# Cross attention with chosen query rows on one core: the order of the loads, of the score weights' spread and of the second choice

## The reference

```python
scores = einsum('bnd,d->bn', x, score_w[0]) + score_b[0]        # x: 8 x 224 x 512
_, topk_idx = top_k(scores, 10)                                  # 10 rows of each input
sparse = take_along_axis(x, topk_idx[:, :, None], axis=1)
q = (sparse @ Wq.T + bq)   # 16 heads of 32
k = (ctx @ Wk.T + bk)      # ctx: 8 x 750 x 512
v = (ctx @ Wv.T + bv)
attn = softmax(q @ k.T / sqrt(32))
out_rows = (attn @ v) @ Wo.T + out_b
return x.at[arange(8)[:, None], topk_idx].set(out_rows)
```

## Time and profile before

| what | value |
|---|---|
| median of 3 timed runs | 142.15 us (142.1 to 142.29) |
| the profiled execution's own time | 141.29 us |
| its span, first to last instruction | 139.5 us |
| mean granted TensorE clock | 0.995 |
| TensorE matmul busy | 132.1 us (95%) |
| VectorE busy | 88.5 us (63%) |
| ScalarE busy | 24.9 us (18%) |
| DMA | 37.52 MB, mean 269 GB/s |

### The profile page before, as it was taken

The page is one execution under the profiler, slowest core; times in us unless marked ns, Lnnn a source line. Parts: engine busy times, 40 slices in busy tenths (PEclk is TensorE's granted clock), DMA queues, the critical chain, the costliest instruction groups (busy, mean ns, idle before and its releaser), DMA issues.

```text
span 139.5 us, 3090 instructions
## 1 busy us (share of the span) xinstructions
PE 132.1 (95%) x1298; PEld 126.2 (90%) x1298; DVE 88.5 (63%) x247; ACT 24.9 (18%) x53; POOL 7.5 (5%) x34
## 2 busy tenths in 40 slices
PE   4989999899999999999999999999999999999980
PEld 2567999789999999999999999999999999999970
DVE  1798696899890577287870575077218799874150
ACT  4122400030322160003140031004101400231110
POOL 7700000003000000000000000000000000000002
PEclk9999999999999999999999999999999999999998
DMA  4999999999997189999989985996691092000001
GB/s 131 415 414 417 409 411 401 444 434 413 416 385 308 46 332 401 271 401 435 427 328 314 318 343 147 318 324 266 222 316 45 5 331 120 0 0 5 0 5 47
DMA packets 6958, 37.52 MB, mean 269 GB/s; under 512 B 961, under 2 KB 961, under 8 KB 4642
## 3 DMA queue, kind: packets, MB, share of 16 engines
q1 hardware_dynamic: 6528, 37.00, 69.7%
q0 software_dynamic: 128, 0.33, 0.7%
q10 hardware_dynamic: 290, 0.01, 0.2%
HBM read 33.50 MB, written 3.83 MB: 268 GB/s over the span
## 4 chain that ended last, share of the span: by engine, by line
PE 72%; DMA 14%; SPq 7%; issue 2%; DVE 1%; POOLq 1%; POOL 0%; DVEq 0%
PE mix_ps L846 38%; PE logits_ps L827 23%; DMA ctx_r<-ctx_rows_dram 14%; PE logits_ps L813 5%; SPq L205 3%; SPq L212 3%; PE logits_ps L785 2%; PE logits_ps L751 1%; PE mix_ps L785 1%; POOLq L60 1%; DVE o_T L610 1%; PE misc_ps L859 1%; DVE heads L607 1%; PE logits_ps L859 0%; SPq L218 0%
## 5 line engine op out<-in xcount | busy, mean ns | idle before, releaser
L846 PE MATMUL mix_ps<-probs,ctx_r 125*128 125x160 f32 x384 | 54.0, 300 | 0.3
L846 PEld LDWEIGHTS mix_ps<-probs,ctx_r 125*128 125x128 f32 x384 | 52.5, 190 | 0.8 <-DMA ctx_r<-ctx_rows_dram 0.4
L827 PE MATMUL logits_ps<-qk,ctx_c 128*125 128x160 f32 x240 | 33.4, 299 | 0.0
L827 PEld LDWEIGHTS logits_ps<-qk,ctx_c 128*125 128x125 f32 x240 | 32.9, 188 | 0.0
L813 PE MATMUL logits_ps<-qk,ctx_c 128*125 128x160 f32 x144 | 20.6, 302 | 0.7 <-DMA ctx_c<-ctx_cols_dram 0.7
L533 DVE TENSOR_REDUCE col_max<-logits_ps 125x160 f32<-125x960 f32 x8 | 9.3, 1157 | 18.8 <-PE logits_ps L827 15.2
L813 PEld LDWEIGHTS logits_ps<-qk,ctx_c 128*125 128x125 f32 x144 | 19.7, 187 | 1.1 <-DMA ctx_c<-ctx_cols_dram 0.9
L361 ACT ACTIVATE mix<-mix_ps 128x320 f32<-128x320 f32 x16 | 7.0, 439 | 62.1 <-PE mix_ps L846 62.1
L572 DVE TENSOR_REDUCE prob_sum<-probs 125x160 f32<-125x960 f32 x8 | 14.7, 1842 | 4.4 <-ACT probs L357 4.4
L357 ACT ACTIVATE probs<-probs 125x480 f32<-125x480 f32 x16 | 9.3, 603 | 30.3 <-DVE probs L565 30.3
L408 DVE CUSTOM_DVE_ANT_0 product<-x_sb,score_w_sb 112x513 f32<-112x513 f32 x16 | 10.4, 692 | 1.3 <-DMA x_sb<-x_lines_dram 1.2
(11 more groups left out here) (130 smaller groups left out, 96.1 us busy)
## 6 DMA issues: line engine op xcount, KB each, us to landing
ctx_r<-ctx_rows_dram SPq DMA_DIRECT2D x8, 1536.0 KB, 8.0
ctx_c<-ctx_cols_dram SPq DMA_DIRECT2D x6, 1500.0 KB, 10.8
x_sb<-x_lines_dram SPq DMA_DIRECT2D x8, 520.0 KB, 9.5
out_dram<-x_sb SPq DMA_DIRECT2D x8, 448.0 KB, 12.8
ctx_c<-ctx_cols_dram SPq DMA_DIRECT2D x2, 750.0 KB, 14.5
ctx_c<-ctx_cols_dram SPq DMA_DIRECT2D x4, 375.0 KB, 15.5
wq_sb<-wq_dram SPq DMA_DIRECT2D x1, 1024.0 KB, 7.5
wk_sb<-wk_dram SPq DMA_DIRECT2D x1, 1024.0 KB, 10.0
```

The source lines that it names most:

```text
L827: last = nc.tensor.matmul(logits_ps[n][0:S_P, t // BANK_T, (t % BANK_T) * HQ:(t % BANK_T + 1) * HQ], ctx_c[n][:, f, t, :], qk[:, b, f, :], ...
L846: last = nc.tensor.matmul(mix_ps[half][:, f * HQ:(f + 1) * HQ], ctx_r[n][0:S_P, t, c:c + P], probs[n][:, t, :], start=(t == 0), stop=(t == ...
```

## The change

There are five edits.

1. Score weights: they came as one line of 512 numbers by ScalarE's queue and were spread over the partitions by four products on TensorE and four copies by VectorE. Now they come as 32 x 16 numbers, first in SP's queue; VectorE turns them with one 32 x 512 transpose, and two copies by VectorE and one by ScalarE fill the other partitions. TensorE's start is two products of 512 columns in one piece, in place of 256 columns, the four products and 512 columns.
2. SP's first loads: `wk` and the columns of contexts 0 and 1 go ahead of inputs that stood before them, and inputs 6 and 7 come last. The rows of context 0 come in two halves, and `weigh_by_part` uses them half by half.
3. VectorE: `name_first` goes ahead of score(3), scores 3 to 5 behind the key dot, scores 6 and 7 behind the softmax of context 0; the choice of inputs 2 to 7 goes behind both softmaxes. TensorE's transpose of the scores moves between the halves of weigh(0).
4. SP's load of the columns of context 3 now also waits for the gather. In weigh(1), `transpose_picked` stands at product 18 (was 14) and `project_queries(1)` at 21 (was 19).
5. `find_max` is done in two halves, so that the first starts when half of the logits are there; `find_shift` handles 10 columns of maxima in place of 5.

```diff
-WARM_WEIGHTS, WARM_SCORES, WARM_RANKS = (256,), (512,), (256, 128)
+WARM_SCORES, WARM_RANKS = (512, 512), (256, 128)
...
+ROW_PARTS = [(0, BANK_T), (BANK_T, S_T)]
...
+            def load_rows_part(k):
+                ts = slice(*ROW_PARTS[k])
+                sp.dma_start(ctx_r[0][:, ts, :], ctx_rows[0, :, ts, :]).then_inc(part_rows_in[k], 16)
...
             sp.wait_ge(logits_done, 2)
+            sp.wait_ge(gathered, 16)
             load_cols(3, 1)
...
-            act.dma_start(score_line[:, :], score_row).then_inc(score_w_in, 16)
...
+            act.wait_ge(score_w_turned, 1)
+            nc.scalar.activation(score_w_sb[3 * QUAD:X_P, 0:D], score_w_sb[0:X_P - 3 * QUAD, 0:D], ACT.Copy).then_inc(high_w_done, 1)
...
+            def turn_score_w():
+                dve.wait_ge(score_w_in, 16)
+                nc.vector.transpose(score_w_sb[0:QUAD, 0:D].rearrange("p (k c) -> p k c", c=QUAD),
+                                    score_cols[:, :].unsqueeze(2).broadcast_to([QUAD, D // QUAD, QUAD])).then_inc(score_w_turned, 1)
+                dve.wait_ge(score_w_turned, 1)
+                for k in range(1, 3):
+                    nc.vector.tensor_copy(score_w_sb[k * QUAD:(k + 1) * QUAD, 0:D], score_w_sb[0:QUAD, 0:D]).then_inc(score_w_done, 1)
+                dve.wait_ge(score_w_done, 2)
+                dve.wait_ge(high_w_done, 1)
...
             def find_max(b, n):
-                dve.wait_ge(logits_done, b + 1)
-                nc.vector.tensor_reduce(col_max[0:S_P, :], tiles(n).rearrange("p k t c -> p c k t"), AX.XY, ALU.max)\
-                    .then_inc(max_step, 1)
+                for k, done in enumerate((first_logits, logits_done)):
+                    dve.wait_ge(done, b + 1)
+                    nc.vector.tensor_reduce(col_max[0:S_P, k, :], tiles(n)[:, k, :, :].rearrange("p t c -> p c t"), AX.X, ALU.max)\
+                        .then_inc(max_step, 1)
...
+            def weigh_by_part():
+                for k, (t0, t1) in enumerate(ROW_PARTS):
+                    pe.wait_ge(part_rows_in[k], 16)
+                    pe.wait_ge(exp_done, k + 1)
+                    if k:
+                        transpose_scores()
+                    for half in range(2):
+                        for f in range(2):
+                            c = (2 * half + f) * P
+                            for t in range(t0, t1):
+                                last = nc.tensor.matmul(mix_ps[half][:, f * HQ:(f + 1) * HQ], ctx_r[0][0:S_P, t, c:c + P],
+                                                        probs[0][:, t, :], start=(f == 0 and t == 0), stop=(t == S_T - 1),
+                                                        skip_group_check=True)
+                        if k:
+                            last.then_inc(mix_ready[half], 1)
...
-            logits_by_step(1, 1, [], {8: transpose_scores})
-            weigh(0, 0, {})
-            weigh(1, 1, {14: transpose_picked, 19: lambda: project_queries(1)})
+            logits_by_step(1, 1, [], {})
+            weigh_by_part()
+            weigh(1, 1, {18: transpose_picked, 21: lambda: project_queries(1)})
```

More of the change, by code:

```diff
@@ L49, with build @@
 TILE = 64
+ROW_PARTS = [(0, BANK_T), (BANK_T, S_T)]
 COL_PARTS = [[(0, 2), (2, 3), (3, 4)], [(0, 1), (1, 2), (2, 4)]]
 EARLY_COPIES = 5
-def build(nc, x, x_lines, ctx_rows, ctx_cols, wq, wk, wv, wo, in_bias, out_b, score_row, out):
+def build(nc, x, x_lines, ctx_rows, ctx_cols, wq, wk, wv, wo, in_bias, out_b, score_turned, out):
     x_rows = x.rearrange("b n d -> (b n) d")
@@ L166, in build @@
         ctx_r_in = [sem(f"ctx_r_in{n}") for n in range(2)]
+        part_rows_in = [sem(f"part_rows_in{k}") for k in range(len(ROW_PARTS))]
         consts_cleared, numbers_done, vec_consts = sem("consts_cleared"), sem("numbers_done"), sem("vec_consts")
@@ L215, in copy_x @@
                 sp.dma_start(out_pairs[:, b, :, :], x_sb[0:X_P, b, :, 0:D]).then_inc(x_copied, 16)
+            sp.dma_start(score_cols[:, :], score_turned).then_inc(score_w_in, 16)
             load_x(0, 3)
             sp.dma_start(wq_sb[:, :, :], wq).then_inc(wq_in, 16)
+            sp.dma_start(wk_sb[:, :, :], wk).then_inc(wk_in, 16)
+            load_cols_part(0, 0)
             load_x(3, 4)
-            sp.dma_start(wk_sb[:, :, :], wk).then_inc(wk_in, 16)
+            load_cols_part(0, 1)
             load_x(4, 5)
-            load_cols_part(0, 0)
+            load_cols_part(0, 2)
             load_x(5, 6)
[L224 to L231, removed]
+            for k in range(len(COL_PARTS[1])):
+                load_cols_part(1, k)
+            load_x(6, 8)
+            load_rows_part(0)
+            load_rows_part(1)
             load_rows(1, 1)
@@ L629, in _ @@
             dve.wait_ge(vec_consts, 5)
[L630 removed]
+            turn_score_w()
             dve.wait_ge(edge_done, 1)
@@ L640, in _ @@
             copy_parts()
-            score(3)
+            name_first()
             dve.wait_ge(bias_in, 16)
@@ L647, in _ @@
             spread_queries(0)
-            score(4)
             spread_key_dot(0)
-            name_first()
-            score(5)
-            score(6)
+            for b in range(3, 6):
+                score(b)
             find_max(0, 0)
-            score(7)
             find_shift(0)
             subtract_max(0, 0)
+            score(6)
+            score(7)
+            find_max(1, 1)
+            find_shift(1)
+            subtract_max(1, 1)
             choose_eight()
@@ L659, in _ @@
             move_idx()
-            find_max(1, 1)
-            find_shift(1)
-            subtract_max(1, 1)
             sum_probs(0, 0)
@@ L684, in keep_warm @@
                                      start=True, stop=True)
[L686 to L690, removed]
             def spread_scores(b):
@@ L816, in logits_by_step @@
                             skip_group_check=True)
+                        if f == DT - 1 and t == BANK_T - 1:
+                            last.then_inc(first_logits, 1)
                 last.then_inc(logits_done, 1)
@@ L829, in logits @@
                             ctx_c[n][:, f, t, :], qk[:, b, f, :], start=(f == 0), stop=(f == DT - 1))
+                    if t == BANK_T - 1:
+                        last.then_inc(first_logits, 1)
                 last.then_inc(logits_done, 1)
+            def weigh_by_part():
[13 more added lines that the diff above has]
+                            last.then_inc(mix_ready[half], 1)
             def weigh(b, n, between):
-                pe.wait_ge(ctx_r_in[n], (b // 2) * 16 + 16)
+                pe.wait_ge(ctx_r_in[n], (b // 2) * 16 + (16 if n else 0))
                 pe.wait_ge(exp_done, 2 * b + 1)
```

29 lines of the change are left out of this document (14 added, 15 removed).

## The result

The change made the kernel slower: 147.07 us (146.23 to 148.71, 4 executions) against 142.12 for the kernel before on the same chip (140.98 to 142.29, 4 executions), a ratio of 1.035 [1.025, 1.044]. The profiled execution took 148.71 us and is the longest of the four (the others: 146.23, 146.45, 147.70). Executions of one kernel lie up to 7 us apart here, and a ratio with an interval is taken from those within 1.5% of the kernel's fastest alone, so it can differ from that of the medians shown.

What follows compares the result with a forecast made beforehand. TensorE bounds the kernel after context 0's rows load, and columns 4 come only just in time (cushion 0.3 us). Gains of -0.43 -1.07 +0.35 overrun by a 2.3 us wait: net +1.2 on 142.15, so 143.35 us, range 141.2 to 145.0.

Steps and rivals of the forecast that it cites:

- Columns 3 behind the gather: SP's queue: the stream waits for the gather, columns 4 land at 72.6, TensorE waits 2.3 us, logits(4) starts 1.2 later.
- Columns and weigh(0): Reordered first loads: columns land without a wait, half of context 0's rows at 29.9 sets weigh(0); weigh(1) gains 1.5 us.
- the small steps: In weigh(1), with `project_queries(1)` at product 21: `fold_pairs` waits 0.3 us, leaving a gain of 1.15.
- The choice and the gather: VectorE's order: gather issued at 38.8 instead of 33.29, takes 2.7 us, lands at 41.5, just before TensorE wants it.
- rival 2: Gather slow by itself at 7.6 us: TensorE waits 4.8 in weigh(1), columns 4 land at 77.5, 148.1 us; chance 0.05.
- Start: Before logits(0): score weights turned by VectorE let score(0) start at 5.05, gaining 0.43 us; logits(0) at 16.2, not 16.64.
- the early steps run at the low clock: One of three cases in rival 3: TensorE's early steps at the low clock; shared total 143.9 to 146 us, chance 0.15.
- rival 3: More is late: clock falls in TensorE's wait, early steps at low clock, or later gather; 143.9 to 146 us, chance 0.15.
- The fall in the wait: Case in rival 3: clock falls in TensorE's wait, a 6.52 us stage takes 13 at 1.2 GHz; shared chance 0.15.

Runs made afterwards that it cites:

- e1: Changed kernel with edit 1 taken back (old spread of score weights, TensorE's old start): 142.22 to 144.56 us, median 143.53, no interval.
- e9: Changed kernel once more, nothing edited: 145.26 us (143.52, 143.58, 146.94, 148.87), ratio 1.012 to the kernel before.
- e6: Changed kernel with edit 1 taken back and three of the five early copies moved behind the load of columns 4: 140.26 us, ratio 0.990.
- e2: Changed kernel with edit 1 taken back and without the wait of columns 3 for the gather: 147.4 us, ratio 1.041.
- e3: Changed kernel, its own start kept, without the wait of columns 3 for the gather: 147.62 us, ratio 1.042.
- e8: Kernel before with only the choice of inputs 2 to 7 moved behind context 1's softmax: 148.94 us, ratio 1.051.
- e4: Changed kernel with a third product of 512 columns at TensorE's start: 143.2 us, ratio 1.011.
- e7: Changed kernel with a third product of 512 columns at the start and three copies moved behind columns 4: 140.68 us, ratio 0.992.
- e15: e7 again, to count late starts: none late in 6; with e7 1 of 15 late, the others 140.42 to 140.95 us.
- e13: e6 again, to count late starts: with e6 2 of 16 at 144 us or more, the others 140.06 to 141.57 us.
- e10: Changed kernel, its own start kept, with three copies moved behind columns 4: 144.09 us (141.20, three from 144.02 to 144.32), no interval.
- e12: e6 with the choice back ahead of context 1's softmax and the transpose of the scores ahead of weigh(0): 143.61 us, ratio 1.010.
- e14: e10 again, to count late starts: 5 of 10 late, the profiled one 145.69 us; with e10 8 of 14 late.
- e5: Kernel before with edit 1 alone: 143.25 us (141.61 to 145.55, 10 executions), ratio 1.003.

## Why the prediction was wrong

- **Columns 3 behind the gather** was right in mechanism and size: a wait of 2.3 us was forecast, 2.04 to 2.27 were measured in e1, e9 and the changed kernel. E6 shows the cause by taking it away: moving three copies brings logits(4) from 72.70 (e1) to 70.30, and the profiled executions from 142.69 to 140.12.
- **Columns and weigh(0), the small steps**: right. In e1 weigh(0) starts at 29.53 (29.9) and `fold_pairs` at 46.61 (46.3). The gather cost a wait of 0.8, where I had an edge; it does not show in the end, since columns 4 set that.
- **The choice and the gather**: right. 3.1 us, near the bound of 2.6, refutes rival 2. What the Trainium skill says (page DMA: Bandwidth & Descriptors, section Queues, rings and completion order), turns between queues packet by packet, would by my reading let the gather lose little in a full stream; the runs have 7.0 to 7.4 us in it (e2, e3, e8) and 3.1 beside an empty queue. The measurement decides: the wait of columns 3 buys 4.6 us (e1 against e2).
- **Start** is the step that failed. It counted -0.43 us, priced by what VectorE waits for, and put the change of TensorE's own start at nothing. VectorE's part came out: the turn took 0.70 (0.6), the two copies 0.92 together, and score(0) starts at 4.72 in the first profile and at 5.09 in e9 (5.05). But with two products of 512 columns in place of 256, the spread and 512, TensorE stands for 1.05 to 2.26 us behind them, where the kernel before worked from 1.1 to 9 us with one gap of 0.7, and the clock is low behind it in all six profiles: until 11.3 to 11.7 us in three of them, until about 20 or 21.5 in the others. In the first profile this puts logits(0) 4.4 us behind the forecast, in e9 1.0. In most executions of the changed kernel (6 of 8 at 146 us or more) the cost is the larger one. Where TensorE is kept at work, logits(0) starts as early as was forecast or nearly (16.2): 15.96 to 16.66 with the third product (e4, e7, e15). The old start does as well with edits 2 to 5 (15.9 to 16.5 in e1, e6, e13), so that the gain ahead of logits(0) cannot be put down to edit 1. I had "the early steps run at the low clock" in rival 3, at 0.15 with 3 us at most, and gave it no working.
- **The fall in the wait** was in rival 3 too. It occurred in the first profile and in e4 (1.9 us each), and not in e1 and e9, with waits of 2.0 to 2.3 us in all four. The forecast of 143.35 therefore holds for the executions without a late start (143.52 and 143.58 in e9) and misses the median by 3.7 us. That these two lie so near it is in part luck: 143.35 is the sum added to the median of 142.15, though the sum came from a profile 0.86 us below, and e9 makes that up by starting logits(0) 1.0 us behind the forecast.

What stays open: why the same start has the clock back at 11.5 us in one execution and only at 20 or later in the next. Edit 1 makes the late one more frequent (8 of 14 against 2 of 16), but the old start has it as well: 12 of 57 executions of the kernel before took 144.07 to 145.67 us too. That these times come from a low clock ahead of logits(0) is inferred; a profile shows it only for the changed kernel, e10, e12 and e14.

## What to carry to other kernels

Before you add a wait to a queue, list what is behind it down to the first load that is only just in time, and move what nobody waits for (here three copies of outputs) behind that load: with the old start it turned 1.4 us above the kernel before into 1.2 us below it, from profile to profile. Price an edit of TensorE's first microseconds by the gaps that it leaves and what the clock does behind them, not by its instructions alone, and time it over ten executions or more, since one profile shows only one of the two courses. A wait of TensorE of 2 us or more cost its length and, in some executions, 3.4 us or more at half clock behind it (1.9 us of time in the first profile and in e4).

## What the runs showed of the hardware

- The rise of TensorE's clock differs between executions of one program: 4.6 us in e9's profile of the changed kernel, 20.0 in the first one; 4.5 to 20.9 over all kernels.
- It can fall again early, in e3, e5 and e9 for some 3.4 us and in e14 from 7.9 to 21.5. In e9 it rose at 4.6 and was low from 8.1 to 11.5, with TensorE busy 3.82 of 4 us:

```profile
8.00:12.00 4.00, 3.82 (x28) 2.27 (x27) 2.87 (x14) 0.61 (x2) 0.00 (x0) 0.57 1.01 421
```

- The granted clock in a row can be wrong until the first change on record. The first profile of the changed kernel shows 1.00 from 16 to 20 us, where the products took nearly twice their time (16 of `fold_keys` in 1.28 us, 0.73 in e9):

```profile
16.00:20.00 4.00, 4.00 (x65) 4.00 (x64) 0.52 (x2) 0.79 (x2) 0.00 (x0) 1.00 1.03 407
```

- It can fall behind a wait. Waits of 2.0 to 2.3 us were followed by a fall in the first profile, e4 and e12 and by none in e1 and e9; waits of 4.8 to 5.1 us by one in e2, e3 and e8.
- An indirect gather of 80 rows of 2 KB takes 3.1 us beside an empty queue and 7.0 to 7.6 in the full stream of another.
